# Epsilon as a third triple of layer-norm statistics, one GpSimd instruction less per pair of tiles, and a new order of all steps

## What is computed

```python
def _layernorm(x, axis=-1, eps=1e-05):
    m = jnp.mean(x, axis=axis, keepdims=True)
    v = jnp.var(x, axis=axis, keepdims=True)
    return (x - m) / jnp.sqrt(v + eps)
...
    x = x + jnp.tanh(g_xattn[0]) * _L0_xattn_ref(_layernorm(x, axis=-1), ctx_1024, ctx_1024, mask_Bx1xSxS2_if1, L0_xattn_Wq, L0_xattn_bq, L0_xattn_Wo, L0_xattn_bo)
    x = x + jnp.tanh(g_ffn[0]) * _L0_ffn_ref(_layernorm(x, axis=-1), L0_ffn_w1, L0_ffn_b1, L0_ffn_w2, L0_ffn_b2)
```

## Time and profile before

| what | value |
|---|---|
| median of 3 runs | 330.82 us (330.63 to 332.22) |
| the profiled execution | 331.0 us |
| its span, first to last instruction | 329.1 us |
| TensorE matmul busy | 310.3 us, 94% |
| VectorE busy | 229.8 us, 70% |
| ScalarE busy | 140.6 us, 43% |
| GpSimd busy | 66.7 us, 20% |
| DMA engines' mean share | 8.4% |
| granted TensorE clock | 0.997 of full speed |

### The profile page before, as it was taken

One profiled execution on the slowest core, in us unless ns is written; L12 is line 12 of the kernel. 1 busy time (PEld: TensorE's weight loads), 2 busy tenths in 40 slices (PEclk: granted clock), 3 DMA queues, 4 the chain that ended last, 5 costly groups with the idle time before them and its releaser, 6 DMA issues.

```text
span 329.1 us, 5834 instructions
## 1 busy us (share of the span) xinstructions
PE 310.3 (94%) x2151; PEld 205.7 (62%) x2151; DVE 229.8 (70%) x640; ACT 140.6 (43%) x294; POOL 66.7 (20%) x115
## 2 busy tenths in 40 slices
PE   8999999997999999999999999999999998898993
PEld 3563553882454468897788355488779774676441
DVE  4986862679932479789886495365656668889995
ACT  1366354222264662253433826523253635665300
POOL 6232350336500200203030302010210501011220
PEclk9999999999999999999999999999999999999998
DMA  6950210001310000000000000000000000000002
GB/s 184 320 175 0 61 38 2 2 1 45 88 51 2 2 0 0 2 1 2 0 2 0 4 0 2 0 2 0 2 0 2 0 3 0 0 3 0 0 1 66
DMA packets 8977, 8.74 MB, mean 27 GB/s; under 512 B 3547, under 2 KB 6901, under 8 KB 8949
## 3 DMA queue, kind: packets, MB, share of 16 engines
q1 hardware_dynamic: 8949, 8.37, 8.4%
HBM read 7.84 MB, written 0.52 MB: 25 GB/s over the span
## 4 chain that ended last, share of the span: by engine, by line
PE 65%; DVE 24%; ACT 6%; issue 2%; POOL 1%; DVEq 0%; ACTq 0%
PE psum L975 59%; DVE mx L1696 5%; DVE wide L1859 2%; PE psum L1066 2%; DVE xn L1569 2%; ACT wide L1374 2%; DVE wide L1866 1%; ACT wide L1502 1%; DVE wide L1865 1%; DVE stats L1560 1%; ACT q L1374 1%; PE psum L1152 1%; DVE xn L1876 1%; DVE xn_t L1875 1%; DVE nmax L1830 1%
## 5 line engine op out<-in xcount | busy, mean ns | idle before, releaser
L1696 DVE TENSOR_REDUCE mx<-psum 128x4 f32<-128x308 f32 x96 | 38.0, 470 | 3.5 <-PE psum L975 3.3
L1374 ACT ACTIVATE wide<-psum 128x512 f32<-128x512 f32 x72 | 36.8, 619 | 7.6 <-PE psum L975 7.3
L975 PE MATMUL psum<-halves 128*128 128x512 bf16 x153 | 38.0, 380 | 0.0
L1374 ACT ACTIVATE q<-psum 128x512 f32<-128x512 f32 (+1 forms) x36 | 21.2, 594 | 35.3 <-PE psum L975 26.9
L913 POOL TENSOR_SCALAR nw<-mv 128x2 f32<-128x2 f32 x32 | 6.9, 217 | 139.5 <-DVE mv L1563 139.5
L975 PE MATMUL psum<-q_hi,first_hi 128*128 128x512 f32 (+1 forms) x68 | 31.0, 456 | 0.0
L975 PE MATMUL psum<-wide 78*128 78x386 f32 (+1 forms) x73 | 25.8, 498 | 3.7 <-DVE wide L1847 2.5
L1569 DVE TENSOR_SCALAR xn<-x,mv,nw 128x128 f32<-128x128 f32 x64 | 20.9, 372 | 9.8 <-POOL nw L914 9.6
L975 PE MATMUL psum<-q_lo,first_hi 128*128 128x512 f32 (+1 forms) x68 | 26.8, 394 | 0.0
L975 PE MATMUL psum<-q_hi,first_lo 128*128 128x512 f32 (+1 forms) x68 | 26.8, 394 | 0.0
L914 POOL TENSOR_TENSOR nw<-nw,minus_half 128x2 f32<-128x2 f32 x32 | 23.4, 732 | 2.7
(11 more groups left out here) (229 smaller groups left out, 562.5 us busy)
## 6 DMA issues: line engine op xcount, KB each, us to landing
early<-in_ffn SPq DMA_DIRECT2D x8, 256.0 KB, 2.8
w_attn<-in_attn SPq DMA_DIRECT2D x1, 640.0 KB, 7.8
w_attn<-in_attn SPq DMA_DIRECT2D x2, 288.0 KB, 6.3
x<-in_x SPq DMA_DIRECT2D x2, 256.0 KB, 3.6
w_ffn<-in_ffn SPq DMA_DIRECT2D x1, 512.0 KB, 7.3
early<-in_ffn SPq DMA_DIRECT2D x1, 512.0 KB, 4.2
out<-x SPq DMA_DIRECT2D x2, 256.0 KB, 2.3
rows<-in_rows SPq DMA_DIRECT2D x1, 468.0 KB, 6.0
```

The costliest lines, as they stand in the source:

```text
L975: return nc.tensor.matmul(out_, lhs, rhs, start=start, stop=stop, **kw)
L1374: A.activation(dst, banks.bank(*name)[0:rows_, 0:cols_], fn, **kw).then_inc(drained["act"], 1)
L1696: last = V.tensor_reduce(mx[:, b, t, lane_heads(g)], banks.bank("max", layer, b, t, g)[:, 0:GK].rearrange("p (h k) -> p h k", k=CTX), AX.X ...
```

## The change

1. `stats` grows from six to nine numbers per row. At the start of VectorE's program two memsets, each waited for, set the third triple once: count 0, mean 0, and epsilon times 128 as count times variance. `bn_stats` still writes the first six; `bn_aggr` now reads nine, so that its variance has epsilon in it.
2. GpSimd's `norm` loses the addition of epsilon and the wait behind it, and reads the variance directly.
3. The planned cost of `norm` on GpSimd goes from 1.0 to 0.72 us.
4. The whole table `LATER` is replaced, and with it the order of steps on all four engines, the dealing of banks and the idle matmuls.

```diff
 LATER = {
-        0: (126, -1967, -204, -171, 1292, -1466, 59, 130, -36, 456, 151, 1308, -193, 1373, 162, 31, 175, -1546, -94,
...
+        0: (-551, -416, -535, -47, 889, -2602, 967, -314, -617, 1, -552, 896, -357, 917, -128, -516, 122, -37, 171,
...
     def norm(stage, after=()):
         for h in range(2):
             step("norm", stage, h, after=list(after) + in_order("dve", "norm", stage, h),
-                 then={"pool": in_order("pool", "norm", stage, h)}, dve=0.65, pool=1.0)
+                 then={"pool": in_order("pool", "norm", stage, h)}, dve=0.65, pool=0.72)
...
-        stats = sb("stats", [P, B, T, 6])
+        stats = sb("stats", [P, B, T, 9])
...
             def norm(b, stage, h):
                 tiles = slice(2 * h, 2 * h + 2)
                 pool.wait_ge(var_ready[b], 2 * stage + h + 1)
-                link(G.tensor_scalar(nw[:, b, 0, tiles], mv[:, b, tiles, 1], LN_EPS, None, ALU.add))
-                G.tensor_tensor(nw[:, b, 2, tiles], nw[:, b, 0, tiles], minus_half[:, tiles], ALU.pow)\
+                G.tensor_tensor(nw[:, b, 2, tiles], mv[:, b, tiles, 1], minus_half[:, tiles], ALU.pow)\
                  .then_inc(xn_rstd_ready[b], 1)
...
-                    last = V.bn_stats(stats[:, b, t, :], x[:, b, t, :])
+                    last = V.bn_stats(stats[:, b, t, 0:6], x[:, b, t, :])
...
             V.memset(idle_t, 0.0).then_inc(idle_made, 1)
+            link(V.memset(stats[:, :, :, 6:9], 0.0))
+            link(V.memset(stats[:, :, :, 8:9], LN_EPS * D))
```

## The result

The changed kernel takes 322.2 us (321.9 to 322.9, 4 runs) beside 331.3 us (330.6 to 332.2, 4 runs) for the kernel before: a ratio of 0.9727, 95% interval 0.9696 to 0.9759. On a second chip it was 322.2 beside 331.6 (0.9719, interval 0.9701 to 0.9736). Forecast were 329.3 us and a range of 325.5 to 333.0.

A forecast was written before the change was run, and what follows sets the result against it. TensorE was taken as the bound from 97 to 254 us, waits on other engines elsewhere. Gains 0.6 + 0.3 + 0.6 = 1.5 us, less under 0.1, took 330.8 to 329.3 us; range 325.5 to 333.0.

The forecast's parts named there:

- I take 0 for the order itself: Whole kernel: the new order of steps was put at 0, with minus 4 to plus 3.5 us as bounds.
- My own sign of being wrong: Two middle stretches: forecast wrong if their 10.2 + 8.8 us of idle matmuls move by more than 2 us either way.
- a better order: Reductions from 78.7 us: other half's feed-forward matmuls run under them, recovering about 3 us, giving 326.3 us; chance 0.18.
- the freed port: At 76 us: normalisation no longer meets a split; 2.9 us gain in all, giving 327.9 us; chance 0.12.
- The port's term: Half 1, stage 2, about 76 us: GpSimd's splits hold up VectorE's normalisation by 1.7 us; gain 0 or 2.0, 0.6 taken.
- the tie: At about 76 us, old order: split starts about 76.15, VectorE arrives about 76.2; gain 0.1 us or 2.0 us.
- The fallback to 0.6 us: Half 1, stage 2: with neither winner given, the second pair's plain latency of 0.6 us was taken, bounds 0 and 2.0.
- The direct term at 258 us: Half 1, stage 6: the chain runs through both additions and powers, so 0.6 us come off.
- At 235 us: Half 0, stage 6, before the GRU's first round: between 0 and 0.6 us of gain, 0.3 taken.
- bn_aggr: VectorE's norms: reading nine numbers costs 3 ns more each, under 0.1 us on the path; by triples 83 ns, 1.7 us.
- At the start: First norm, before the first transposes: gain 0, as ScalarE's table load and keys are late next; at most 0.6 us.
- The rival on the slower side: Splits and key parts land beside VectorE operations needing the port, 1.7 us per meeting, giving 332.7 us; chance 0.20.

The follow-up runs named there:

- The order alone: The changed kernel with the norm as before (GpSimd adds epsilon in its own instruction, six statistics): 324.5 us, ratio 0.9792 to the kernel before.
- the edit alone: The kernel before with only the norm's edit (nine statistics, no addition on GpSimd), table, planned cost, banks and idle matmuls unchanged: 332.2 us beside 331.6.
- the old table with the new cost: The kernel before with the norm's edit and planned cost 0.72 us, keeping the old table LATER without a search: 338.4 us, ratio 1.0213.
- the idle matmuls dealt anew: The kernel before with the norm's edit, its old order kept, banks and idle matmuls planned again for a 0.72 us norm: 330.7 us, ratio 0.998.
- the four kernels that keep the meeting at 76 us: The norm's edit with: nothing else, 332.2 us; idle matmuls replanned, 330.7; old table and new cost, 338.4; old order before 105 us then new, 332.3.
- splits early: Old order with the norm's edit and replanned idle matmuls, splits 3 and 4 moved some 20 us earlier on ScalarE and GpSimd: 328.3 us, ratio 0.9864.
- the three mixes that begin with the new order: The norm's edit, changed kernel's order for steps planned before a cut, old order after: cut at 75 us, 327.5 us; at 105, 324.5; at 250, 324.5.
- the one with the new tail: The mix of new order before 250 us and old after, with VectorE's last 27 steps also in the changed kernel's order: 323.6 us, ratio 0.9754.
- the early table load: The changed kernel with one small activation at the start of ScalarE's program, loading its table while x is on its way: 322.1 us beside 322.2.

## Why the prediction was wrong

**The step that failed is "I take 0 for the order itself".** The order alone brought 7.1 us, 6.2 beside executions in which the clock didn't fall. I had bounds of minus 4 and plus 3.5 for it and gave minus 3 a chance of 0.18. The bound was drawn too tight from my own rows: they held 10.2 + 8.8 us of idle matmuls in the middle stretches, the port's 1.7 us, and a tail of 16 us in which VectorE sets the pace, and I allowed an order 4 us at best. The new one took 4.0 us of idle matmuls from the first stretch, and 2.3 from the second and the tail together. My own sign of being wrong, a move of more than 2 us in the two middle stretches, did show: they went from 19.0 to 14.0. The argument "the order before came from a like search with almost the same costs" was an argument from how the kernel was made, not from the profile, and it was wrong. The idle matmuls in the trace were the better witness.

**The rival "a better order" was right in kind and named the place.** I had 3 us for half 0's other work under the 32 reductions. It was 3.0 us, and that the numbers meet is luck: what the traces show under the reductions is scores, not the feed-forward matmuls that I had in mind. And I had treated it, the freed port, and the tail as alternatives, each with its own time, where one new order took all of them at once: 2.4, 3.0, 2.3. Within an order that was searched as a whole the gains of different stretches add, so the low end of the range had to be their sum.

**The port's term.** The price of 1.7 us was right, and so was the tie: in the old order the split won by 0.11 us, and the term was 0. VectorE and GpSimd, then, don't meet at semaphores alone. What I left out is what follows on TensorE: a pause of 2.1 us with no idle matmuls in it, as the plan doesn't know of it, and then in part of the executions a lower clock. The fallback to 0.6 us ("the plain latency") fits neither branch.

The Trainium skill's page "SBUF — State Buffer" ("SBUF: two separate sides") has the two engines exclude each other on shared ports for whole instructions. The traces agree: the pair of tiles takes 2.32, 2.47 and 0.59 us with two splits, with two splits and with none beside it, and 0.92 us with the 0.59 us split beside it, and in the first two cases it ends within 0.1 us behind the second split.

**The direct term at 258 us** was 0.1 in the old order, not 0.6: the transposes sat in TensorE's queue behind 24 matmuls of the other half. I had read the chain, which does pass through both powers, but not TensorE's list in that window. A chain tells what was last; it doesn't tell how close the next was. At 235 us it was 0 in the old order. In the new order the two places bring 0.6 and 0.4 us, near my 0.6 and 0.3, but two that I had at nothing bring as much: half 1's norm of stage 1 at 60 us (0.6), and the last norm (0.4). So all of the edit together brings 2.3 us there instead of my 1.5.

**bn_aggr** takes 174 ns instead of 166: 8 ns for three numbers more, not 3, and far from 83. In all 64 x 8 = 0.5 us of VectorE. With the edit alone:

```profile
L1562 DVE BATCH_NORM_AGGREGATE mv<-stats 128x2 f32<-128x9 f32 x64 | 8.5, 174 | 1.1
```

The two memsets: no trace of them in the time.

**At the start** the term 0 was right and its reason only half right: what is late next is mostly VectorE behind the mask's DMA, and ScalarE's table load only where the mask lands early.

**The rival on the slower side** (more meetings on the path) didn't come, but the new order isn't free of meetings. Two of VectorE's key operations are held up in it beside GpSimd, off the path that sets the time:

```profile
24.29 1.41 DVE L1609 TENSOR_TENSOR k_lo<-k_t,k_hi 128x154 fp32r<-128x154 f32 x1
...
26.34 1.25 DVE L1608 CAST k_hi<-k_t 128x154 fp32r<-128x154 f32 x1
...
24.25 1.28 POOL L921 TENSOR_TENSOR x<-x,gbias 128x512 f32<-128x512 f32 x1 [0.78 <-DVE xn L1568]
25.79 1.71 POOL L893 TENSOR_TENSOR keys_lo<-k_lo,lane_mask 128x616 fp32r<-128x616 f32 x1 [0.26 <-DVE k_lo L1609]
```

Alone they take 0.32 and 0.23 us. The first was held up in the kernel before too, at 25.95, the second wasn't. So the count of meetings went from two to three, counting the one with the short split. What changed is that the dear one in front of the reductions is gone. That an order can be much slower is shown by the old table with the new cost, 6.8 us slower. But it has the same one long pair as the kernel before (2.46 us) and no more, so it isn't slower by more meetings; by what, no run took apart.

Open is why the clock falls in some executions of one and the same kernel and not in others, and how the last 1.4 us divide within the GRU rounds, which no run took apart. That the scores between the reductions are what brings the 3.0 us is argued, not shown.

## What to carry to other kernels

Where engines run fixed lists, an edit is worth what the list lets through: the same edit brought 0.2 us at most in one order (0.9 with the idle matmuls dealt anew) and 2.3 us in another, and a table of priorities made for other costs lost 6.8 us. To bound what a new order may bring, add up the idle matmuls and waits by stretch, and let the stretches add, though halves of two orders joined together don't; don't trust that an earlier search has found them. Before crediting a shorter latency, look at what stands in the next engine's queue just ahead of the reader, and put the long instructions of GpSimd where VectorE doesn't need the shared port.

## What the runs showed of the hardware

TensorE's clock reacted to a pause, and not always. In the kernel before and in the four kernels that keep the meeting at 76 us and were profiled, TensorE stands still for 2.1 to 2.3 us at about 77 us. In the profiles of these four the granted clock was at the lower level (1.2 GHz) for 3.4 us in three and 6.8 us in the fourth, from 0 to 1.6 us behind the end of that pause; in the profile of the kernel before it stayed up, but it fell in others of its executions:

| executions of the kernel before, by mean granted clock | us |
|---|---|
| 0.996 to 0.998 | 330.5 to 331.6 |
| 0.992 to 0.994 | 331.5 to 332.6 |
| 0.987 | 333.2 |
| 0.982 | 334.6 to 335.4 |

The kernels without that pause (the order alone, splits early, the three mixes that begin with the new order, the one with the new tail, the early table load, the changed kernel) show 0.995 to 1.0 in every run, and spreads of 0.5 to 1.3 us where the kernel before has 4.9. So removing one hidden collision also made the time steadier. A fall costs some 1.2 us, an idle matmul 380 ns at the full clock; whether idle matmuls in that pause would have kept the clock up, no run shows.
